# Last feed-forward of a two-layer decoder: the first activation and the first product of a tile change places with the shift and the rounding of the tile before

## The reference, cut to what matters

```python
def _quant_act(x):
    s = max(abs(x), axis=-1, keepdims=True) / 127.0 + EPS
    return clip(round(x / s), -128.0, 127.0), s

def _qlinear(x, w):
    wq, ws = _quant_weight(w)
    xq, xs = _quant_act(x)
    return einsum('bsi,oi->bso', xq, wq) * xs * ws

gate = silu(_qlinear(x, w_gate))            # 512 -> 2048
up = _qlinear(x, w_up)                      # 512 -> 2048
x = layernorm(x + _qlinear(gate * up, w_down))   # 2048 -> 512
```

## Time and profile before

| | us |
|---|---|
| median of 3 timed runs | 2950.88 (2943.35 to 2951.95) |
| profiled execution, its own time | 2926.72 |
| span of the trace in it | 2925.0 |
| busy over the span: PE, DVE, ACT, POOL | 2687.7, 1805.9, 1409.8, 316.3 |
| first to last product of this stage (line 2786) | 2703.8 to 2903.8 |

### The profile page before, as it was taken

One profiled execution on the slowest core, in us unless ns is written; L12 is line 12 of the kernel. 1 busy time (PEld: TensorE's weight loads), 2 busy tenths in 40 slices (PEclk: granted clock), 3 DMA queues, 4 the chain that ended last, 5 costly groups with the idle time before them and its releaser, 6 DMA issues. The chain is left out here.

```text
span 2925.0 us, 40483 instructions
## 1 busy us (share of the span) xinstructions
PE 2687.7 (92%) x12665; PEld 1678.4 (57%) x12686; DVE 1805.9 (62%) x3459; ACT 1409.8 (48%) x2965; POOL 316.3 (11%) x405
## 2 busy tenths in 40 slices
PE   8999997978999986998998999996999999997887
PEld 4454554445588863776776777774545454533443
DVE  5665674654443336755755756753777777874676
ACT  4454452322133322553652652742577676764554
POOL 0230003000711113001001001002110101000000
PEclk9999998989999998999999999998999999998999
DMA  4393104741687754223233223211000000002000
GB/s 151 71 108 80 43 14 152 275 154 49 202 273 242 241 181 163 95 102 103 72 107 111 66 101 115 66 65 58 5 5 6 5 6 2 2 2 87 8 22 29
DMA packets 114166, 266.24 MB, mean 91 GB/s; under 512 B 14464, under 2 KB 37008, under 8 KB 113200
## 3 DMA queue, kind: packets, MB, share of 16 engines
q1 hardware_dynamic: 97152, 211.16, 21.9%
q0 software_dynamic: 16816, 52.64, 7.9%
HBM read 208.97 MB, written 58.48 MB: 91 GB/s over the span
## 5 line engine op out<-in xcount | busy, mean ns | idle before, releaser
L2451 DVE TENSOR_REDUCE x_neg_max<-bank 128x1 f32<-128x512 f32 x512 | 327.4, 684 | 95.9 <-PE bank L2296 95.4
L2403 ACT ACTIVATE x_weights<-bank 128x512 f32<-128x512 f32 x512 | 279.1, 600 | 127.0 <-PE bank L2307 122.1
L1826 ACT ACTIVATE a_probs<-bank,a_neg_max 128x128 f32<-128x128 f32 (+3 forms) x256 | 135.9, 531 | 241.7 <-DVE a_neg_max L1916 237.6
L1726 PE MATMUL bank<-a_x_high,a_weights 128*128 128x512 f32 x640 | 219.2, 406 | 9.2 <-DVE a_x_low L1848 4.5
L109 PEld LDWEIGHTS bank<-all_ident,a_probs 128*128 128x128 f32 x1200 | 151.4, 140 | 84.2 <-issue 44.7
L109 PE MATMUL bank<-all_ident,a_probs 128*128 128x128 f32 x1200 | 193.4, 273 | 2.2 <-ACT a_probs_t L1818 2.2
L1761 PE MATMUL bank<-a_k_cols,a_q_cols 128*128 128x128 f32 (+3 forms) x512 | 176.8, 434 | 0.3
L1818 ACT COPY a_probs_t<-bank 128x128 f32<-128x128 f32 (+3 forms) x256 | 107.4, 420 | 144.2 <-PE bank L109 144.0
L1790 PE MATMUL bank<-a_wo,a_att_high 128*128 128x512 f32 x512 | 162.3, 398 | 4.7 <-DVE a_q_cols L1865 2.9
L1451 DVE TENSOR_TENSOR moe_acc<-bank,moe_acc 128x512 f32 x79 | 54.6, 692 | 170.7 <-PE bank L1117 170.5
L1106 PE MATMUL bank<-moe_gh_cols,moe_item 128*128 128x256 f32 x632 | 151.9, 384 | 2.5 <-DMA moe_item<-moe_items 2.2
(11 more groups left out here) (407 smaller groups left out, 5538.4 us busy)
## 6 DMA issues: line engine op xcount, KB each, us to landing
a_weights<-split_qkv SPq DMA_DIRECT2D x80, 512.0 KB, 3.6
moe_item<-moe_items SPq DMA_DIRECT2D x79, 257.0 KB, 3.6
moe_item<-moe_items SPq DMA_DIRECT2D x79, 256.0 KB, 3.5
a_wo<-split_out SPq DMA_DIRECT2D x8, 2048.0 KB, 7.9
a_wo<-split_out SPq DMA_DIRECT2D x16, 1024.0 KB, 10.2
split_qkv<-x_qkv_parts SPq DMA_DIRECT2D x12, 1024.0 KB, 5.6
moe_items<-in_L_ffn_e_w POOLq DMA_DIRECT2D x40, 256.0 KB
split_out<-a_turned SPq DMA_DIRECT2D x8, 1024.0 KB, 4.4
```

What stands on the lines that cost most here:

```text
L1726: last = pe.matmul(mm[g % 2], weight[:, k, :], x[:, k, :], start=n == 0, stop=n == 3 * KD - 1)
L1826: act.activation(probs[:, n % SLOTS, 0:t], sc[n % 4][:, 0:t], ACT.Exp, bias=neg_max[:, n:n + 1], accum_out=row_sum[:, n:n + 1]).then_inc(s ...
L2403: act.activation(weights[:, chunk % 2, k, :], weight_banks[slot % 2], ACT.Exp).then_inc(s.weight.free, 1)
L2451: dve.tensor_reduce(neg_max[:, g % 2, j, h:h + 1], score_banks[slot % 3], AX.X, ALU.max, negate=True) \
```

## The change

On ACT the shift of tile t-1 goes from the head of step t to between silu 0 and silu 1 of tile t. On DVE the rounding of tile t and the normalisation of tile t-2 go from the end of step t to between product 0 and product 1 of step t+1. In the steps without a tile of their own (t = 16, 17) both stand at the head of the step, and a last `finish` follows the loop. The instructions, their number, shapes, operands and semaphores are the same; PE, POOL and SP are not touched.

```diff
+            def shift_h(t, slot):
+                act.wait_ge(s.h_top, t + 1)
+                act.activation(shifted_h[:], inner[:, slot, :], ACT.Identity, bias=round_col[:],
+                               scale=inv_h[:, slot:slot + 1]).then_inc(s.h_shifted, 1)
+
             def step(t, slot):
                 other = 1 - slot
-                if 1 <= t <= LAST + 1:
-                    act.wait_ge(s.h_top, t)
-                    act.activation(shifted_h[:], inner[:, other, :], ACT.Identity, bias=round_col[:],
-                                   scale=inv_h[:, other:other + 1]).then_inc(s.h_shifted, 1)
+                if t == LAST + 1:
+                    shift_h(LAST, other)
                 if t <= LAST:
                     for c in range(COLS):
+                        if c == 1 and t >= 1:
+                            shift_h(t - 1, other)
                         act.wait_ge(s.ga.full, t * COLS + c + 1)
...
             def step(t, slot):
                 at = slice(slot, slot + 1)
+                if t > LAST:
+                    finish(t - 1, 1 - slot)
                 if t <= LAST:
                     for c in range(COLS):
+                        if c == 1 and t >= 1:
+                            finish(t - 1, 1 - slot)
                         dve.wait_ge(s.up.full, t * COLS + c + 1)
...
                 if t <= LAST:
                     dve.tensor_scalar(step_down[:, at], step_h[:, at], w.scale[:, 2:3], None, ALU.mult)
+
+            def finish(t, slot):
+                if t <= LAST:
                     dve.wait_ge(s.h_shifted, t + 1)
                     if t >= 2:
                         dve.wait_ge(s.tq.full, h_bank(t - 2, 1) + 1)
                     dve.tensor_scalar(quant_h[:, slot, :], shifted_h[:], ROUND_INT, 127.0, ALU.subtract, ALU.min).then_inc(s.h_ready, 1)
                 if t >= 2:
+                    x = m.x_tok[:, t - 2, :]
                     dve.wait_ge(s.rstd_ready, t - 2 + 1)
-                    dve.tensor_scalar(x, x, st.mean_var[:, slot, 0:1], st.rstd[:, at], ALU.subtract, ALU.mult).then_inc(s.x_done, 1)
+                    dve.tensor_scalar(x, x, st.mean_var[:, slot, 0:1], st.rstd[:, slot:slot + 1], ALU.subtract, ALU.mult).then_inc(s.x_done, 1)
...
             pipeline(dve, step)
+            finish(LAST + 2, LAST % 2)
```

## The result

The changed kernel takes 2929.43 us (median of 7 runs, 2923.0 to 2935.32), the one before 2944.59 (7 runs, 2941.72 to 2951.95) in the same series. The medians lie 15 us apart. The ratio worked out from all these runs is 0.9943, with a 95% interval of 0.9929 to 0.9956, which makes 17 us less, between 13 and 21. Forecast were 18.4 us less.

The account below looks back on a forecast made before the run. PE in the stage before the output was taken to be held up by a loop through ACT's shift and DVE; 1.74 + 1.73 + 13 x 1.15 = 18.4 us off 2950.88 gave 2932.5 us, range 2920 to 2944.

Parts of the forecast that it names:

- What bounds the kernel, and the loop: Stage before the output: PE stands still 1.79 us a step, both releases hanging on the shift; step 13.27 to 12.13 us.
- ACT: ACT's queue in a steady step: silu 0 starts at 1.57 us, shift 0.59 later; the 0.86 us standstill before G2 goes.
- DVE: DVE's queue in a steady step: rounding at 4.30, product 1 at 5.89, U3 at 6.69 us; a 0.65 us standstill stays.
- Steps 1 and 2: The stage's first two steps with a shift, worked out separately: U3 comes 1.74 and 1.73 us sooner.
- The sum: Whole stage: 1.74 + 1.73 + 13 x 1.15 = 18.4 us less, taken off the median 2950.88 for 2932.5 us.
- The bound for two new neighbours: Shift after silu on ACT, product beside shift on DVE: 1.05 to 1.17 us a step; 4 us allowed in all.
- Table loads: Rival on ACT: more switches to Silu cost table loads, 7 us slower, 2958; chance 0.02 together with the clock rival.
- PE's clock: Rival on PE: its greater share, 95%, lowers the clock; below 0.91 all is given back; 0.02 together with table loads.
- The wait gone whole: Rival in the steady step: PE never stands still, 1.79 us a step, together 27.5 us, 2923.4 us; chance 0.05.
- The signs of being wrong: Four signs: step over 12.8 us, G3 waits, shift waits for the inverse beyond steps 1 and 2, another stage moves.

Follow-up runs that it names:

- e3: The changed kernel with the normalisation moved behind product 1, the rounding left in front of it: 2922.17 us, ratio 0.9927 to the kernel before.
- e9: The changed kernel with each rounding done twice in a row, DVE emptied in between: 2951.17 us, ratio 1.0009 to the kernel before.
- e1: The kernel before with only ACT's half of the change, silu 0 in front of the shift: 2955.09 us, ratio 1.0038.
- e2: The kernel before with only DVE's half, rounding and normalisation between product 0 and product 1: 2938.73 us, ratio 0.9982.
- e6: The changed kernel with rounding and normalisation between product 1 and product 2: 2897.47 us, ratio 0.9917, beside 2921.28 us of the kernel before.
- e11: The kernel of e1 once more, unaltered: one time 2958.9 us, stage 210.8 us.
- e10: The kernel of e1 with each rounding done twice in a row: 2994.63 us (2 runs), ratio 1.0152 to the kernel before.

## Why the prediction was right

- *What bounds the kernel, and the loop.* Right. The steady step was forecast at 12.13 us and is 12.12 to 12.13. e3 and e9 show that the named way (rounding, normalisation, product 1, U3) is on the loop that sets it, one for one; e1 and e2 that ACT's and DVE's waits are one loop.
- *ACT.* Right: silu 0 starts 1.57 us after G0, the shift 0.58 behind it (0.59 forecast), silu 1 1.99 after that, and G3 does not wait (U2 at 2793.98, G3 at 2794.84).
- *DVE.* Right: product 0 starts at 2.37 us, 0.07 later than forecast, which nothing waits for; rounding at 4.28 after G0 (4.30), product 1 at 5.88 (5.89), U3 at 6.69 (6.69). The bound for two new neighbours, a product beside a shift, was not needed: the shift still takes 2.10 us and the product 0.75.
- *Steps 1 and 2.* Forecast 1.74 and 1.73 us less; from 10.51 and 10.50 to 8.79 and 8.77, that is 1.72 and 1.73. In step 2 G0 itself comes 0.19 us sooner after the U3 before it (2.39 for 2.58) and U3 later after G0 (6.39, forecast 6.2), which the forecast did not have and which cancels from U3 to U3.
- *The sum.* Forecast 18.4 us, in the stage 18.5: 1.72 + 1.73 + 13 x 1.15, and 0.1 in step 0, which runs in part at the lower clock. By time 17 (13 to 21). The level is right in part by luck: the 2932.5 was taken off the first median of before, 2950.88, which with more runs came to 2944.59, 6 us lower; that the changed kernel is only 3 us under the forecast, at 2929.43, is because the medians lie 15 us apart and not 18.
- *The rivals.* Table loads: there is one in the stage after too (1.28 us, in front of the first silu), although the stream now changes twice a step. PE's clock: 1.00 over the steady part, so PE's greater share of 96% cost nothing; it is the longer standstill of e1, not the fuller PE, that brings the clock down. The wait gone whole needs another order: e6 has it.
- *The signs of being wrong.* Three stayed away (step over 12.8 us, G3 waits, shift waits for the inverse beyond steps 1 and 2). The fourth, another stage that moves by more than a few us, did turn up between the two profiled executions: the last stage starts 21 us later. It doesn't speak against the forecast, since traces of the same kernel differ as much (2703.8 and 2720.9 for before, 2725.1 and 2692.5 for after); it was a sign that can't be read from one trace each.

## What to carry to other kernels

Before an order is changed on two engines, follow the loop once round and ask which wait is late next; here each half alone was worth +0.58 or -0.42 us a step and both -1.15. An operation for which nobody waits (the normalisation, 0.45 us) costs its whole length when it stands on that loop, and nothing one place later. If the whole time scatters by 10 to 20 us and a step of the stage repeats to 0.02, read the step.

## What the runs showed of the hardware that was not expected

A standstill of PE can cost more than its length: from 2.36 us a step on, the granted clock fell behind some of them, at 1.68 us each. In each line the idle time of PE (start to start, less 0.87 us) and what the clock did:

| kernel | standstills of a step, us | clock granted in the steady part |
|---|---|---|
| before | 0.86 and 0.93 | 1.00 |
| changed | 0.64 | 1.00 |
| e9 | 1.94 | 1.00 |
| e1, e11 | 2.36 | 0.98, a drop in 2 of 13 steps |
| e10 | 3.67 | 0.91, a drop in 11 of 13 steps |

Between 1.94 and 2.36 us nothing was measured. Nor is it shown that one long standstill is worse than two short ones of the same sum: before (two, 1.79 us) and e9 (one, 1.94 us) both stay at 1.00, and no kernel here has two of 2.36 us together in its steady steps. The standstill also lies before U2 in e1 and e10 and before U3 in e9.

The Trainium skill, "TensorE: Matmul & The Clock Gate" (section "HAM oscillation — how this bites in real kernels"), tells of a clock that falls back after each wait on DMA between bursts of matmuls, about 3 to 5 us long. The runs agree in kind, and show it here for waits on DVE, from a standstill of 2.36 us on, at a price of 3 us in the stage of e1.
